# Count tables of the first mean layer stored in five parts, four pairs apart

## The chip, the cores and the metric

The kernel runs on one core of a Trainium2 chip. The metric is the time of one execution on the device in microseconds (us), the median of several runs. TensorE (PE in the profile), VectorE (DVE), ScalarE (ACT), GpSimd (POOL) and SyncE (SP) each follow their own list of instructions and meet in semaphores.

## What is computed

Four graph layers run one after the other on a graph of 3125 nodes with 128 features and 53125 edges sorted by destination: a gated layer, a mean layer, an attention pair and a pair of mean layers with normalisation. The change touches the second, whose sum over the edges is

```
deg = segment_sum(ones_like(dst), dst, n); deg = maximum(deg, 1.0)
agg = segment_sum(feat[src], dst, n)
h = feat @ W_self + b_self + agg / deg[:, None] @ W_neigh
x = layernorm(x + h)
```

The last two layers sum the same way, `segment_sum(x[src], dst)`, over the same edges.

## The kernel before, in words

**No gather, but counts.** The sum over edges is a product with a matrix that counts, for each source node and each destination node, the edges between them. Edges are sorted by destination, so a run of edges meets few destinations. The 104 batches of 512 edges are cut into pairs of 256 edges (208 pairs), and 26 pairs make one *table* (`SBP = 26`): for every source node (25 tiles of 128, `NT`) a row of 428 destination columns (`M_COLS`) in bf16. A table is 128 partitions x 25 x 428 values, 21400 bytes in each partition. There are 8 tables (`NSB`), the last one in two blocks of 18 and 8 pairs. Three tables fit on chip (`TABS = 3`, tile `counts`).

**The stage** is `mean_build` (L1677). For each pair n, VectorE makes one-hot matrices (`make_lo`, `make_wide`, `make_onto`, three pairs ahead), TensorE multiplies them (`count`, L1832 to L1835) into one of four banks, and ScalarE copies the bank into the table at the pair's own column (`copy_counts`, L1777 to L1783) and increments `copied`. A bank is free again when its copy is done, so TensorE can be some pairs ahead of ScalarE and no more. While table k is being counted, TensorE multiplies table k-1 with the features split in three bf16 parts (`apply`, L1850), some three matmuls after each pair, and VectorE adds the result to `acc` (`add_dense`, L1926, with a register load of the table's origin at L1920).

**Registers.** The column of each pair is known at run time only. ScalarE loads the 26 columns of a table into registers in one instruction (`loaded_starts`, L753 to L758, called at L1806 when `n % SBP == 0`):

```
if n % SBP == 0:
    values = loaded_starts(mybir.EngineType.Activation, place_m[0:1, n:n + SBP], M_COLS - WP)
```

The attention stage does the same with 14 columns a table (`place_a`), on ScalarE and on VectorE, beside the row gathers of GpSimd.

**The stores.** The last two layers need the same tables, so each one is written to DRAM (`count_tabs`) when it is finished, by `keep(s)` on SP (L1739 to L1741): it waits for `copied >= 26 (s+1)` and issues one transfer of 2675 KB, which increments `table_stored[s % 3]` by 16. ScalarE's `clear(k)` (L1767 to L1775) sets a column strip of the next table to zero in the middle of the table before; from the fourth table on it waits for the store of the table that had the buffer. The `update` stage that follows (L679 to L682) waits on SP for all stores. At the end of `mean_build` SP, TensorE and VectorE each load the value `rounds` (L1239).

Nothing else is issued on SP in the stage but three weight loads at its start. The order on each engine is the order in which the Python code issues; the semaphores do the rest. The names that the steps of the prediction use are `keep`, `clear`, `copy_counts`, `loaded_starts`, `place_m`, `copied` and `table_stored`.

Of the kernel before, what the change touches and what calls it, by code (L numbers as in the profile page):

```python
# [41 lines left out]
NSB, AT_DENSE = 8, 7  # L42
# [8 lines left out]
def build_program(nc, a, out):  # L51
# [9 lines left out]
    NT = -(-(N + W) // P)  # L61
# [127 lines left out]

    first_ad = dram("first_ad", [NB * BE + NODES, 1])  # L190
    count_tabs = dram("count_tabs", [NSB, P, NT * M_COLS], BF16)
    TABS = 3
    table_stored, table_in = [sem(f"table_stored{i}") for i in range(TABS)], [sem(f"table_in{i}") for i in range(2)]
    aux_rows = dram("aux_rows", [NB * BE, 4])
    tables = [dram(f"table{i}", [NODES, P]) for i in range(5)]
# [468 lines left out]
    def update(name):  # L664

        with phase(name) as (sb, sem):
            a_made, summed = sem("a_made"), sem("summed")
            v, normed, normed_d = sem("v"), sem("normed"), sem("normed_d")
            count, variance, root, deviation, by_act, by_dve, rstd_ready = norm_parts("n", sb, sem)
            w_n = wide_w[:, P:2 * P]  # L670
            ZB = 6

            def by_engine(g):

                return CHUNKS[1][0] <= g and (g - CHUNKS[1][0]) % 2 == 1

            with nc.Block() as block:  # L677
                @block.sync
                def _(sp):  # L679
                    clear_spent(sp)  # L680
                    for k in range(TABS):
                        sp.wait_ge(table_stored[k], 16 * len(range(k, NSB, TABS)))  # L682

                @block.tensor
                def _(pe):
                    for g in range(NG):
                        reach(pe, summed, tiles_to(g - ZB) if g >= ZB else 0)
                        for n, t in enumerate(GROUPS[g]):
                            mm = pe.matmul(bank[g % ZB][:, n * P:(n + 1) * P], acc[:, t * P:(t + 1) * P], w_n, start=True, stop=True)
                        mm.then_inc(a_made, 1)  # L690

                @block.scalar
                def _(act):
                    for c in range(2):
                        root(act, c)
                        act.wait_ge(rstd_ready, c + 1)
                        for g in range(*CHUNKS[c]):
                            if not by_engine(g):
                                for t in GROUPS[g]:
                                    by_act(act, x_sb, y_sb, t).then_inc(normed, 1)  # L700

                @block.vector
                def _(dve):
                    link = chain(dve, v)
                    def mean(g):
                        dve.wait_ge(a_made, g + 1)
                        for n, t in enumerate(GROUPS[g]):
                            dve.scalar_tensor_tensor(out=y_sb[:, t, :], in0=bank[g % ZB][:, n * P:(n + 1) * P],
                                                     scalar=rdeg[:, t:t + 1], in1=y_sb[:, t, :],
                                                     op0=ALU.mult, op1=ALU.add).then_inc(summed, 1)  # L710

                    def measure(g):
                        dve.wait_ge(summed, tiles_to(g))
                        count(dve, y_sb, g)

                    for g in range(NG):
                        mean(g)
                        if g >= 1:
                            measure(g - 1)
                            if g - 1 == CHUNKS[0][1] - 1:  # L720
                                variance(dve, link, 0)
                            elif g - 1 == CHUNKS[0][1]:
                                deviation(dve, link, 0)
                    measure(NG - 1)
                    variance(dve, link, 1)
                    deviation(dve, link, 1)
                    dve.wait_ge(rstd_ready, 2)
                    for g in range(*CHUNKS[1]):
                        if by_engine(g):
                            for t in GROUPS[g]:  # L730
                                by_dve(dve, x_sb, y_sb, t).then_inc(normed_d, 1)
# [945 lines left out]
    def mean_build(name, table, x_from, w_self, w_neigh, b):  # L1677

        with phase(name) as (sb, sem):
# [56 lines left out]
            with nc.Block() as block:  # L1736
                @block.sync
                def _(sp):
                    def keep(s):  # L1739
                        sp.wait_ge(copied, (s + 1) * SBP)  # L1740
                        sp.dma_start(count_tabs[s, :, :], flat(counts[:, s % TABS, :, :])).then_inc(table_stored[s % TABS], 16)  # L1741

                    clear_spent(sp)
                    sp.wait_ge(a_made, NG)
                    load_self(sp)
                    for s in range(NSB):
                        keep(s)
                    sp.wait_ge(flagged, 1)
                    with only_when(sp) as R:
                        store_rows(sp, table, x_from, tabled)  # L1750
                        fall_sp(sp, R)
# [13 lines left out]
                @block.scalar  # L1765
                def _(act):
                    def clear(k):  # L1767
                        first, _, width, at = M_BLOCKS[k]
                        s = home(first)
                        reach(act, applied, s - TABS + 1)  # L1770
                        if s >= TABS:
                            act.wait_ge(table_stored[s % TABS], 16 * (s // TABS))
                        rest_from, rest_to = at + width - REST, M_COLS if k < LEAP else at + width
                        act.copy(counts[:, s % TABS, :, rest_from:rest_to],
                                 zero[:, 0:1].rearrange("p (a b) -> p a b", a=1).broadcast_to([P, NT, rest_to - rest_from])).then_inc(cleared, 1)  # L1775

                    def copy_counts(n, values):  # L1777
                        act.wait_ge(counted, n + 1)
                        if opens(M_BLOCKS, n):
                            act.wait_ge(cleared, sum(block[0] <= n for block in M_BLOCKS))  # L1780
                        reach(act, copied, n)
                        act.copy(counts[:, home(n) % TABS, :, bass.ds(values[n % SBP], WP)],  # L1782
                                 BANKS_C[n % CR][:, 0:NT * WP].rearrange("p (t w) -> p t w", w=WP)).then_inc(copied, 1)  # L1783

                    def sigmoid(g):
                        act.wait_ge(summed, tiles_to(g))
                        act.activation(sig[:, cut(g), :], y_sb[:, cut(g), :], ACT.Sigmoid).then_inc(sig_ready, 1)

                    def normalise(g):
                        act.wait_ge(rstd_ready, 1 if g < CHUNKS[0][1] else 2)  # L1790
                        for t in GROUPS[g]:
                            by_act(act, x_from, y_sb, t).then_inc(normed, 1)

                    def cast_part(g, k):
                        if k == 0 and by_engine(g):
                            act.wait_ge(normed_d, normed_to(DVE_GROUPS, g))
                        elif k == 0:
                            act.wait_ge(normed, normed_to(ACT_GROUPS, g))
                        cast(act, g, k)

                    act.wait_ge(nothing, 1)
                    clear(0)
                    clears = {first + size // 2: k + 1 for k, (first, size, _, _) in enumerate(M_BLOCKS) if k + 1 < LAST}
                    for n in range(NDD):
                        if n % SBP == 0:
                            values = loaded_starts(mybir.EngineType.Activation, place_m[0:1, n:n + SBP], M_COLS - WP)  # L1806
                        if n in SPLIT_AT:
                            cast_part(*SPLIT_AT[n])
                        if n - 1 in SELF:
                            copy_self(act, SELF[n - 1])  # L1810
                        if n == CLEAR_AT:
                            act.copy(acc[:, :], zero[:, 0:1].broadcast_to([P, NODES])).then_inc(acc_clear, 1)
                        if n in clears:
                            clear(clears[n])
                        copy_counts(n, values)
                        if n < NG:
                            sigmoid(n)
                        if n in ROOT_AT:
                            root(act, ROOT_AT[n])
                        for g in NORMALISE.get(n, ()):  # L1820
                            normalise(g)
# [920 lines left out]
```

## Time and profile before

| what | us |
|---|---|
| median of 3 runs | 2037.59 (2037.51 to 2041.03) |
| the profiled execution, its own time | 2039.3 |
| its span | 2037.5 |
| granted clock of TensorE, mean | 0.91 |
| count stage with stores of tables | about 677 to 970 |
| first and last store issued | 741.4, 963.0 |

The span is the time from the first to the last instruction that the profiler recorded; the execution's own time is 1.8 us longer. Times inside the trace are us from the span's start. "Idle before" in a timeline stands in brackets behind an instruction, with what ended it; "issue" is time in which the engine waited for nothing that the profile shows. Register loads (TENSOR_LOAD) are not counted as busy, and stand under the engine's sequencer (ACTq, DVEq). A granted clock of 1.00 is 2.4 GHz, one of 0.50 is 1.2 GHz.

### The profile page before, as it was taken

To read this page: it belongs to the slowest core of one execution; us is meant where nothing else is said; L and a number is where in the kernel's file an instruction comes from. 1 tells how busy PE (TensorE), PEld (TensorE's weight loads), DVE (VectorE), ACT (ScalarE), POOL (GpSimd) and SP (SyncE) were. 2 spreads that over 40 slices of the span, in tenths; PEclk is the share of its full clock that TensorE was granted. 3 is DMA by queue.
4 is the path that set the end of the run, shared out by engine and by line. 5 is a ranking of instruction groups with operands and counts; after the bars stand their busy time and mean duration, and the time that the engine had idled before them with its cause. 6 is when DMAs were issued, how large, how long until landed. Compare 5 with 4: busy or idle time off the path is not lost. (4 is left out here: it accounts for less than half of the span.)

```text
span 2037.5 us, 42968 instructions
## 1 busy us (share of the span) xinstructions
PE 1742.0 (85%) x13651; PEld 1405.7 (69%) x13651; DVE 1412.8 (69%) x4286; ACT 911.7 (45%) x2490; POOL 983.6 (48%) x998
## 2 busy tenths in 40 slices
PE   5799999999999558888466999967599999299996
PEld 5699999999998425445464878757467878166664
DVE  5687788888886778885667766655676664744656
ACT  2566667676665266664303544421154453411100
POOL 3776777777774300000356777735577775300000
PEclk9799999999999759999768999986699999699998
DMA  6988788888884011222352111107221111344542
GB/s 191 269 241 240 235 240 255 256 249 246 255 255 148 7 55 55 109 109 89 127 143 62 45 41 43 45 15 200 70 67 41 41 43 37 123 162 180 198 163 87
DMA packets 145067, 276.87 MB, mean 136 GB/s; under 512 B 28295, under 2 KB 88333, under 8 KB 141556
## 3 DMA queue, kind: packets, MB, share of 16 engines
q1 hardware_dynamic: 104526, 191.58, 29.2%
q0 software_dynamic: 35456, 79.88, 14.5%
q10 hardware_dynamic: 4854, 2.55, 0.5%
q8 instruction: 118, 1.93, 0.4%
q14 instruction: 113, 0.93, 0.1%
HBM read 228.82 MB, written 45.08 MB: 134 GB/s over the span
## 5 line engine op out<-in xcount | busy, mean ns | idle before, releaser
L959 POOL DMA_INDIRECT gated_rows<-p_tab,src_idx x416 | 429.7, 1033 | 176.0 <-issue 104.4
L1351 POOL DMA_INDIRECT ring<-table,src_idx x384 | 384.1, 1000 | 146.4 <-issue 93.0
L2159 PE MATMUL bank<-counts,mean_xs 128*128 128x416 bf16 (+2 forms) x1350 | 219.5, 321 | 32.0 <-DVE mean_xs L1671 32.0
L1000 PE MATMUL bank<-gated_wide_q,gated_comb 128*128 128x256 f32 x832 | 216.8, 384 | 0.0
L1157 DVE TENSOR_TENSOR gated_pre<-bank,gated_rows 128x512 f32<-128x512 f32 x208 | 142.8, 687 | 101.8 <-PE bank L1000 101.8
L2159 PEld LDWEIGHTS bank<-counts,mean_xs 128*128 128x128 bf16 x1350 | 126.2, 98 | 116.1 <-issue 34.4
L1482 ACT COPY attention_counts<-bank 128x475 f32 (+1 forms) x224 | 127.2, 568 | 176.3 <-PE bank L1506 153.4
L1517 PEld LDWEIGHTS bank<-attention_counts,h_sb 128*128 128x128 f32 x900 | 157.5, 190 | 62.3 <-ACT attention_counts L1482 3.8
L1073 ACT ACTIVATE gated_sig<-gated_pre 128x512 f32<-128x512 f32 x208 | 131.1, 630 | 154.1 <-DVE gated_pre L1157 152.0
L1517 PE MATMUL bank<-attention_counts,h_sb 128*128 128x232 f32 (+1 forms) x900 | 191.9, 341 | 2.3 <-DVE attention_counts L1574 1.7
L1506 PE MATMUL bank<-attention_wide_b,scratch 128*128 128x400 f32 x448 | 189.5, 505 | 0.0
L1782 ACT CAST mean_counts<-bank 128x500 f32 x208 | 124.4, 598 | 103.5 <-PE bank L1835 48.7
L1505 PE MATMUL bank<-attention_wide_a,scratch 128*128 128x300 f32 x448 | 158.2, 435 | 11.6 <-DVE attention_wide_b L1566 5.7
L1000 PEld LDWEIGHTS bank<-gated_wide_q,gated_comb 128*128 128x128 f32 x832 | 143.5, 193 | 11.1
L1463 ACT ACTIVATE scratch<-scratch,w_tab 128x64 f32<-128x64 f32 x384 | 102.2, 336 | 102.1 <-DVE scratch L1551 102.1
L1850 PE MATMUL bank<-mean_counts,mean_xs 128*128 128x416 bf16 (+2 forms) x675 | 142.6, 332 | 3.3 <-ACT mean_counts L1782 2.7
L2345 POOL IOTA attend_spare_at<- 128x25 f32 x1 | 0.2, 162 | 282.2 <-POOLq L677 282.2
L1019 PE MATMUL bank<-gated_w,gated_siluT 128*128 128x128 f32 x832 | 126.4, 274 | 0.0
L1886 DVE TENSOR_TENSOR mean_lo<-lo_iota,src_lo 128x256 bf16<-128x256 bf16 x208 | 87.4, 420 | 46.7 <-PE bank L1835 46.2
L1557 DVE TENSOR_TENSOR scratch<-lo_iota,src_lo 128x256 f32<-128x256 bf16 x224 | 93.5, 418 | 33.4 <-PE bank L1506 23.6
L1032 PE MATMUL bank<-gated_hot,gated_msg 128*128 128x64 f32 x832 | 115.9, 262 | 0.1
L1574 DVE TENSOR_TENSOR attention_counts<-attention_counts,bank 128x25 f32 x206 | 40.5, 197 | 108.8 <-ACT attention_counts L1482 108.4
(428 smaller groups left out, 4018.7 us busy)
## 6 DMA issues: line engine op xcount, KB each, us to landing
counts<-count_tabs SPq DMA_DIRECT2D x16, 2675.0 KB, 9.9
h_sb<-in_edge_attr_dram SPq DMA_DIRECT2D x51, 512.0 KB, 4.9
count_tabs<-mean_counts SPq DMA_DIRECT2D x8, 2675.0 KB, 7.8
gated_relr<-rel_rows SPq DMA_DIRECT2D x104, 128.0 KB
gated_ids<-id_rows SPq DMA_DIRECT2D x26, 512.0 KB
gated_wide_q<-q_tab SPq DMA_DIRECT2D x208, 64.0 KB
attend_hot_lo<-low_hots SPq DMA_DIRECT2D x52, 256.0 KB, 3.3
gated_ea<-in_edge_attr_dram SPq DMA_DIRECT2D x51, 256.0 KB
```

Source lines behind the costliest of these rows:

```text
L959: pool.indirect_dma_start(out=rows[:, q % TICKS, c, :], out_offset=None, in_=p_tab, in_offset=bass.IndirectOffsetOnAxis(ap=src_idx[:, b, j ...
L1000: mm = pe.matmul(PRE[q % 2][:, c * 2 * P:(c + 1) * 2 * P], comb[:, u, k, c, :], wide_q[:, u, c, :], start=True, stop=True)
L1019: mm = pe.matmul(M[:, c * P:(c + 1) * P], siluT[:, q % 2, c, :], w2[:, :], start=False, stop=True, skip_group_check=True)
L1073: act.activation(flat(sig[:, q % 4, :, :]), flat(pre[:, q % 2, :, :]), ACT.Sigmoid).then_inc(sig_ready, 1)
L1157: dve.tensor_tensor(flat(pre[:, q % 2, :, :]), PRE[q % 2][:, :], flat(rows[:, q % TICKS, :, :]), ALU.add).then_inc(pre_ready, 1)
L1351: pool.indirect_dma_start(out=rows[:, n % RING, j, :], out_offset=None, in_=table, in_offset=bass.IndirectOffsetOnAxis(ap=src_idx[:, gathe ...
L1482: act.copy(counts[:, home(n), :, skip:A_COLS][:, :, bass.ds(values[n % ATP], WP - skip)], frm[:, :, skip:WP]).then_inc(copied, 1)
L1505: pe.matmul(to[:, :, 0:WA], lo[:, n % LR, 0, :], wide_a[:, n % WR, :], start=True, stop=False, skip_group_check=True)
L1506: pe.matmul(to[:, :, OFF:WP], lo[:, n % LR, 1, :], wide_b[:, n % WR, :], start=False, stop=True, skip_group_check=True).then_inc(counted, 1)
L1517: mm = pe.matmul(BANKS_D[k % 2][:, 0:width], h_sb[:, m, :], counts[:, home(first), m, at:at + width], start=(m == 0), stop=(m == NT - 1), ...
L1850: mm = pe.matmul(BANKS_D[k % 2][:, 0:width], xs[:, m // 3, m % 3, :], counts[:, home(first) % TABS, m // 3, at:at + width], start=(m == 0) ...
L2159: mm = pe.matmul(BANKS_D[q % ND][:, 0:width], xs[l][:, m // 3, m % 3, :], counts[:, s % 2, m // 3, at:at + width], start=(m == 0), stop=(m ...
```

## The change

A table is stored in five transfers of five node tiles each (535 KB, 4280 bytes in each partition). Part i waits for `copied >= 26 (s+1) + 4 i`, or for all 208 pairs if that is less, so the first part is issued where the whole table was, and the others 4, 8, 12 and 16 copies later, while the next table is being filled. A finished table now counts 80 on its semaphore.

```diff
--- before.py
+++ after.py
@@ -189,7 +189,9 @@
 
     first_ad = dram("first_ad", [NB * BE + NODES, 1])
     count_tabs = dram("count_tabs", [NSB, P, NT * M_COLS], BF16)
-    TABS = 3
+    TABS, PARTS, APART = 3, 5, 4
+    assert NT % PARTS == 0
+    STORED = 16 * PARTS
     table_stored, table_in = [sem(f"table_stored{i}") for i in range(TABS)], [sem(f"table_in{i}") for i in range(2)]
     aux_rows = dram("aux_rows", [NB * BE, 4])
     tables = [dram(f"table{i}", [NODES, P]) for i in range(5)]
@@ -679,7 +681,7 @@
                 def _(sp):
                     clear_spent(sp)
                     for k in range(TABS):
-                        sp.wait_ge(table_stored[k], 16 * len(range(k, NSB, TABS)))
+                        sp.wait_ge(table_stored[k], STORED * len(range(k, NSB, TABS)))
 
                 @block.tensor
                 def _(pe):
@@ -1737,8 +1739,11 @@
                 @block.sync
                 def _(sp):
                     def keep(s):
-                        sp.wait_ge(copied, (s + 1) * SBP)
-                        sp.dma_start(count_tabs[s, :, :], flat(counts[:, s % TABS, :, :])).then_inc(table_stored[s % TABS], 16)
+                        for i in range(PARTS):
+                            sp.wait_ge(copied, min((s + 1) * SBP + APART * i, NDD))
+                            part = slice(i * NT // PARTS, (i + 1) * NT // PARTS)
+                            sp.dma_start(count_tabs[s, :, part.start * M_COLS:part.stop * M_COLS],
+                                         flat(counts[:, s % TABS, part, :])).then_inc(table_stored[s % TABS], 16)
 
                     clear_spent(sp)
                     sp.wait_ge(a_made, NG)
@@ -1769,7 +1774,7 @@
                         s = home(first)
                         reach(act, applied, s - TABS + 1)
                         if s >= TABS:
-                            act.wait_ge(table_stored[s % TABS], 16 * (s // TABS))
+                            act.wait_ge(table_stored[s % TABS], STORED * (s // TABS))
                         rest_from, rest_to = at + width - REST, M_COLS if k < LEAP else at + width
                         act.copy(counts[:, s % TABS, :, rest_from:rest_to],
                                  zero[:, 0:1].rearrange("p (a b) -> p a b", a=1).broadcast_to([P, NT, rest_to - rest_from])).then_inc(cleared, 1)
```

The order of SP's queue in this stage before the change (the rows are DMA issues and what follows them; `rounds` is the value loaded at the stage's end):

```order
L769 DMA wide_w<-in_L_gnn_W_neigh_dram 128x128
L770 DMA wide_w<-in_L_gnn_b_self_dram 128x128
L1741 DMA count_tabs<-mean_counts 128x10700 [waits mean1_copied] x8
L1239 TENSOR_LOAD rounds [waits mean1_flagged]
L1240 COMPARE_AND_BRANCH
```

And with the change:

```order
L771 DMA wide_w<-in_L_gnn_W_neigh_dram 128x128
L772 DMA wide_w<-in_L_gnn_b_self_dram 128x128
L1745 DMA count_tabs<-mean_counts 128x2140 [waits mean1_copied] x40
L1241 TENSOR_LOAD rounds [waits mean1_flagged]
L1242 COMPARE_AND_BRANCH
```

Eight stores of 10700 values in each partition became forty of 2140; what stands before and behind them is the same. On the other engines no instruction is added, taken away or moved.

## Rows read from the trace of the kernel before

**Rows 1.** The page: span and busy time of the engines, whole program.
```profile
span 2037.5 us, 42968 instructions
PE 1742.0 (85%) x13651; PEld 1405.7 (69%) x13651; DVE 1412.8 (69%) x4286; ACT 911.7 (45%) x2490; POOL 983.6 (48%) x998
```

**Rows 2.** Windows from one store of a table to the next (us from the start).
```profile
core 0: us, PE busy (x) PEld busy (x) DVE busy (x) ACT busy (x) POOL busy (x), PEclk, DMA share, GB/s
815.40:846.80 31.40, 23.48 (x152) 13.36 (x152) 23.34 (x96) 16.79 (x27) 0.00 (x0) 0.89 0.21 89
846.80:869.90 23.10, 22.15 (x152) 12.65 (x152) 22.62 (x93) 16.64 (x27) 0.00 (x0) 1.00 0.29 120
```

**Rows 3.** Waits in the count stage, 735 to 985 us: in total, times, longest.
```profile
ACT mean_counts L1782 <- issue: 39.4, 4, 9.9
PE bank L1832 <- ACT mean_counts L1782: 21.8, 3, 7.6
```

**Rows 4.** Timelines of ACT, then PE, 814 to 828 us: start, length, instruction, idle before.
```profile
825.23 0.57 ACT L1782 CAST mean_counts<-bank 128x500 f32 x1 [9.86 <-issue]
...
826.06 0.20 PE L1832 MATMUL bank<-mean_onto,mean_lo 128*128 128x25 bf16 x1 [7.55 <-ACT mean_counts L1782]
```

**Rows 5.** Loads of place_m on ACT (xcount, ns min/median/max): all from 735 us, then the first.
```profile
L755 ACTq TENSOR_LOAD <-place_m x7: 2698/10141/10264, 740.8 to 923.4; - x7
...
L755 ACTq TENSOR_LOAD <-place_m x1: 10222/10222/10222, 740.8 to 740.8; - x1
```

**Rows 6.** Timeline of SP's queue: the store of the third table.
```profile
815.40 0.32 SPq L1741 DMA_DIRECT2D count_tabs<-mean_counts  x1
```

**Rows 7.** Windows inside a long register load (740.8 on) and a short one (788.9).
```profile
740.80:742.20 1.40, 0.79 (x4) 0.27 (x3) 1.40 (x7) 0.57 (x1) 0.00 (x0) 0.50 0.00 0
742.20:748.90 6.70, 2.03 (x8) 0.66 (x6) 2.67 (x12) 0.00 (x0) 0.00 (x0) 0.75 0.97 409
788.90:790.20 1.30, 0.00 (x0) 0.00 (x0) 1.30 (x6) 0.00 (x0) 0.00 (x0) 1.00 1.24 527
```

**Rows 8.** Loads of one value on DVE, all and two of them; first load of place_m.
```profile
L1920 DVEq TENSOR_LOAD <-origin_m x9: 302/889/912, 794.5 to 963.7; - x9
...
L1920 DVEq TENSOR_LOAD <-origin_m x2: 302/303/304, 954.9 to 956.5; - x2
...
L755 ACTq TENSOR_LOAD <-place_m x1: 1933/1933/1933, 677.5 to 677.5; - x1
```

**Rows 9.** Attention stage: ACT's second and third load of place_a.
```profile
L755 ACTq TENSOR_LOAD <-place_a x1: 3037/3037/3037, 1113.6 to 1113.6; - x1
...
L755 ACTq TENSOR_LOAD <-place_a x1: 1236/1236/1236, 1146.3 to 1146.3; - x1
```

**Rows 10.** DMA issues, page and 1000 to 1090 us: count, KB, us to landing.
```profile
count_tabs<-mean_counts SPq DMA_DIRECT2D x8, 2675.0 KB, 7.8
...
table<-h_sb SPq DMA_DIRECT2D x2, 576.0 KB, 3.9
```

**Rows 11.** Register loads of rounds, 960 to 975 us.
```profile
L1239 SPq TENSOR_LOAD <-rounds x1: 511/511/511, 963.4 to 963.4; - x1
...
L1239 PEldq TENSOR_LOAD <-rounds x1: 916/916/916, 966.8 to 966.8; - x1
L1239 DVEq TENSOR_LOAD <-rounds x1: 927/927/927, 968.4 to 968.4; - x1
```

**Rows 12.** Windows after two idles of PE, and the shorter idle in PE's timeline.
```profile
774.80:778.20 3.40, 3.40 (x15) 2.63 (x16) 0.68 (x3) 1.03 (x2) 0.00 (x0) 0.50 0.00 0
...
822.60:826.00 3.40, 0.00 (x0) 0.00 (x0) 0.00 (x0) 0.60 (x2) 0.00 (x0) 0.50 0.00 0
826.00:829.40 3.40, 3.34 (x14) 1.64 (x15) 1.85 (x7) 2.75 (x5) 0.00 (x0) 0.50 0.02 5
829.40:832.80 3.40, 3.40 (x27) 2.09 (x26) 2.92 (x13) 2.36 (x5) 0.00 (x0) 1.00 0.01 2
...
774.79 1.43 PE L800 MATMUL bank<-wide_w,cur 128*128 128x128 f32 x5 [2.75 <-ACT cur L793]
```

## Prediction

> **What bounds the kernel now.** I read the page first: 2037.5 us of span, TensorE busy 85% [rows 1]. Section 4 traces only the end of the program, so I went to the stage that is changed. The windows by table come next [rows 2]: the time from one store of a count table to the next alternates between 31.4 and 23.1 us, for the same 26 pairs and the same TensorE work (23.48 us busy and 22.15 us). So every second table loses 8.3 us. In the short ones TensorE (22.15 of 23.10) and VectorE (22.62) are both nearly full: those have nothing to give. The loss is named in the list of waits of this stage [rows 3]: ScalarE's copy of counts stands 39.4 us, in 4 idles of about 9.9 us, on "issue", which is nothing that the list can name. Its timeline [rows 4] shows one of them: the copy that opens a table starts at 825.23 after 9.86 us of idle, and TensorE starts again at 826.06, after 7.55 us, waiting for ScalarE.
>
> What fills the 9.86 us is a register load, the TENSOR_LOAD of 26 values of `place_m` at L755, which the loop on ScalarE makes when n is a multiple of 26 [rows 5]. There are seven such loads after the first; the median is 10141 ns, the most 10264, the least 2698. With seven of them and the median at 10141, four are long, and four idles are listed: those that open tables 1, 3, 5 and 7, counted from 0 (the one of table 1 took 10222 ns; I take 10.2 us). Those that open 2, 4 and 6 took 2.7 us.
>
> The store of the table just finished is issued by the same event, the 26th copy: SP issues it at 815.40 [rows 6], where ScalarE's idle begins (825.23 less 9.86 us). The windows around the first long load [rows 7] show the transfer: nothing from 740.8 to 742.2, then 6.7 us at 409 GB/s with all 16 DMA engines taken (share 0.97), and 6.7 x 409 is 2.74 MB, the whole table, so it is over at 748.9. The load runs from 740.8 to 751.1 and holds that transfer whole. My reading is that **a register load advances slowly while the transfer runs**.
>
> Other register loads speak for it [rows 8]. VectorE's loads of one value, `origin_m`, of which one follows behind most stores, take 889 ns in the median and 912 at most, and 304 ns at 954.9, where nothing moves. And the first load of 26 values, at 677.5 without a transfer, takes 1933 ns, where the equally short ones take 2698 ns with the last 1.3 us of them in a transfer (the one that ends at 790.2, with a transfer from 788.9 [rows 7]).
>
> **How long would a long load be alone?** No row has it, so I bound it. From below: 1.4 us of it lie ahead of the transfer and 2.2 us behind it [rows 7], so at least 3.6 us. From above: 10.2 us. The nearest rows are the attention stage's loads of 14 values, which alternate in the same phase: 3037 ns at the second, 1236 ns at the third [rows 9]; the program's offsets are 56 bytes times an odd or even number there, 104 bytes times the same here. With 0.30 us for one value, another costs (3.04 - 0.30)/13 = 0.211 us at odd places and (1.24 - 0.30)/13 = 0.072 at even ones; the load at 677.5 gives (1.93 - 0.30)/25 = 0.065 for even ones with no transfer about, 10% less than beside the gathers of the attention stage. So the long load alone is 0.30 + 25 x 0.211 = 5.6 us, or 5.1 us with the 10% taken off. I take **5.4 us**. The stretch is then 10.2 - 5.4 = 4.8 us in 6.7 us of transfer, 0.72 us for each.
>
> The Trainium skill (Runtime: NRT & Kernel Launch, section Instruction fetch mechanics) gives about 200 ns a register for such a load; by that one it would be 5.2 us, the saving per load below 4.0 us in place of 3.8, and the sum 16 us. The row of 1933 ns for 26 values contradicts it for even offsets.
>
> **The change, part by part.**
> 1. The first fifth of a table is stored where all of it was, at the same copy. A fifth is 535 KB; at the measured 409 GB/s it moves in 1.34 us. It starts and hits the load where the whole did, and stretches it by 1.34 x 0.72 = 0.96 us. The load is then 5.4 + 1.0 = 6.4 us, and 3.8 us less than 10.2.
> 2. That load is on the path: TensorE's idle of 7.55 us is the load less 2.7 us that its three spare banks cover, and the table is 8.3 us longer for it [rows 2, 4]. After the change TensorE's idle is about 6.4 - 2.7 = 3.7 us. **4 loads x 3.84 us = 15.4 us.**
> 3. The three short loads have 1.3 us in a transfer. The first fifth covers just that: nothing gained, nothing lost.
> 4. The four further fifths start 4, 8, 12 and 16 copies later, about 3.5 us apart in a short table. They are on SP's queue; the load holds ScalarE, so no copy is counted before it ends, and none of these can meet it. No other register load of ScalarE lies there. VectorE's one-value loads (9 of them, median 889 ns [rows 8]) mostly come some 1.8 us after the store, when the first fifth is nearly through; each may be 0.3 us shorter, and between 0 and 2 us in all would follow. I take 0, since the last of the fifth may still meet them.
> 5. Costs: 32 more issues on SP. One issue takes 0.33 us [rows 6], and SP has nothing else to do in this stage; the order of rows shows it queues only the load of `rounds` behind them. ScalarE's clears wait on `table_stored`, now for the last fifth: that is issued 16 copies later, and the clear that wants the buffer comes 39 copies after the first, so some 23 copies (20 us) remain for a transfer that lands in 7.8 us at full size [rows 10]. Nothing.
> 6. The last table: all five waits are at 208, so five transfers start together where one did. TensorE's and VectorE's loads of `rounds` (916 and 927 ns [rows 11]) fall into them as before. SP's own load, 511 ns at 963.4, comes some 2 us later and ends before TensorE's at 966.8. Nothing.
> 7. TensorE's clock. In the idle of 7.55 us it falls to 0.50 at 822.6, for 6.8 us, of which 3.4 are idle and 3.4 work: 14 matmuls at 0.50, 27 at 1.00, a loss of 1.6 us [rows 12]. After an idle of 2.75 us (ends 774.79) it stands at 0.50 for 3.4 us, all of it on work (15 matmuls). An idle of 3.7 us lies between. If it falls as it ends, for 3.4 us, the cost is the same as now, and I take 0. Bounds: no fall, 1.6 us less for each of 4; or 6.8 us at half all on work, 1.6 us more for each.
>
> Sum: 2037.5 - 15.4 = 2022.1 us of span. The profiled execution took 2039.3 us, its span and 1.8 us around it; the median of the three runs is 2037.59, and against it I forecast **2022.2 us**.
>
> The Trainium skill (DMA: Bandwidth & Descriptors, section Bandwidth) speaks against the edit: it wants transfers of 1 MiB or more for three quarters of the peak, and 535 KB is under that. The row at hand is a store of 576 KB, which lands in 3.9 us [rows 10], where 2675 KB take 7.8.
>
> **Ends of the range.** From that row: a full store lands 1.1 us after its 6.7 us of moving, so 576 KB move in 2.8 us at most. With that and the long load at 5.6 alone (stretch 4.6/6.7 = 0.69 a us), it would be 7.5 us and 2.7 saved, 10.8 in all; with the clock's worse bound (+6.4) that is 2033. At the other end reads stand still in a transfer, the load alone is 3.6 us, 6.6 x 0.8 = 5.3 us are saved each time, 21.1 in all: 2016.5, and with the clock's better bound (-6.4) 2010. Both ends at once on either side are unlikely: I give **2013 to 2031**.
>
> **Rivals.**
> - *Reads stand still during a transfer* (0.09): 2016.5 us. For it: the four long loads are alike. Against: the short load ended at 790.2, in the midst of a transfer that began at 788.9 [rows 7].
> - *The shorter idle costs as much clock* (0.08): 6.8 us at half lie wholly on work; 2022.2 + 6.4 = 2028.6 us.
> - *The change doesn't do what it says* (0.05): the loads are long by their odd offset alone, transfer or not, and keep 10.2 us; TensorE waits as before: 2037.6 us. Against: 14 values at odd offsets take 3.04 us, and 25 of 0.211 make 5.6 us, not 10.2; VectorE's 889 against 304 ns.
> - *Slower* (0.03): a fifth takes as long as a whole, because its cost lies in its pieces (one per partition, 4280 bytes in place of 21400) and not in its bytes. Then a table's five take 33.5 us of transfer while a table lasts 27.2 on average (the mean of a long and a short one), the first fifth still spans the load (nothing saved), and the stores fall behind until ScalarE's clears wait for the buffer: the fifth table's last part would end 5 x 33.5 = 167.5 us after the first store, and is wanted after 5 x 27.2 + 13.6 = 149.6 us. That is 18 us late: 2055.6 us. It decides from (149.6/25 =) 6.0 us a fifth. The 3.9 us landing of 576 KB speaks against it.
>
> The forecast's own case keeps 0.75. All chances but the last two are faster by over 0.2% (4.1 us, about what a measurement of this kernel tells from no change): faster 0.92, within 0.05, slower 0.03.
>
> **What the profile after would show.** The four long loads of `place_m` at 6.4 us (5.0 if reads stand still, 10.2 if nothing helps), the three short ones still at 2.7; ScalarE's idle on "issue" down from 39.4 to about 24 us; TensorE's four idles at 3.5 to 4.5 us; long tables of 27.5 us beside short ones of 23; five bursts of some 1.3 us a table, 40 issues landing in 2.5 to 4 us. I am wrong if the long loads stay over 8 us, if the clock stands at half for more than 4 us of work behind each, or if a later stage gives the gain back.

## The result and the profile after

| what | before | with the change |
|---|---|---|
| median of the runs compared, us | 2038.10 (5 runs) | 2025.19 (5 runs, 2022.09 to 2027.98) |
| ratio | | 0.9927, 95% interval 0.9906 to 0.9949 |
| span of the profiled execution, us | 2037.5 | 2023.9 |

The forecast was 2022.2 us in a range of 2013 to 2031. A later comparison of the same kernel gave 2020.24 us and a ratio of 0.9912 (0.9897 to 0.9926). The whole interval lies below 0.998 both times: faster. Ratios, here and below, compare executions in the chip's normal state alone; one execution of the last kernel below took 6199 us, for a reason that nothing here shows, and its ratio leaves it out.

The page of the kernel after, span and busy times, against [rows 1]: the engines do the same work as before, in 13.6 us less.

```profile
span 2023.9 us, 43000 instructions
PE 1743.0 (86%) x13651; PEld 1407.0 (70%) x13651; DVE 1414.0 (70%) x4286; ACT 912.9 (45%) x2490; POOL 982.3 (49%) x998
```

Windows from one store's first issue to the next, against [rows 2] (columns as there):

```profile
core 0: us, PE busy (x) PEld busy (x) DVE busy (x) ACT busy (x) POOL busy (x), PEclk, DMA share, GB/s
816.26:843.91 27.65, 23.54 (x152) 13.37 (x152) 23.45 (x97) 16.81 (x27) 0.00 (x0) 0.94 0.25 101
843.91:866.91 23.00, 22.06 (x152) 12.65 (x152) 22.92 (x95) 16.64 (x27) 0.00 (x0) 1.00 0.30 120
866.91:894.51 27.60, 23.54 (x152) 13.36 (x152) 22.37 (x92) 16.93 (x27) 0.00 (x0) 0.94 0.25 100
894.51:917.37 22.86, 21.87 (x152) 12.81 (x152) 22.54 (x94) 16.61 (x27) 0.00 (x0) 1.00 0.30 122
917.37:950.63 33.26, 30.38 (x222) 19.72 (x223) 21.25 (x80) 16.70 (x27) 0.00 (x0) 1.00 0.21 84
```

The short tables last 23.0 and 22.86 us, as before. The long ones have gone from 31.4 to 27.65 and 27.60 us. The last window is that of the last table, which is counted in two blocks; the same window of the kernel before, not among the rows above, is:

```profile
924.07:963.05 38.98, 32.26 (x222) 20.35 (x223) 21.69 (x82) 16.66 (x27) 0.00 (x0) 0.91 0.17 72
```

It is 5.7 us shorter, and its clock is 1.00 for 0.91.

Waits of the count stage, against [rows 3]:

```profile
ACT mean_counts L1787 <- issue: 24.2, 4, 6.1
PE bank L1837 <- ACT mean_counts L1787: 11.1, 4, 3.8
```

ScalarE's idle on "issue" fell from 39.4 to 24.2 us, TensorE's wait for ScalarE in this list from 21.8 (3 waits) to 11.1 (4 waits, the fourth of 0.7 us). TensorE's idle at the first of the four tables stands in another row, that of the copy `cur`: 8.17 us before, 4.62 after. The timelines of ScalarE and TensorE at the same table, against [rows 4]:

```profile
822.26 0.58 ACT L1787 CAST mean_counts<-bank 128x500 f32 x1 [6.03 <-issue]
...
823.09 0.18 PE L1837 MATMUL bank<-mean_onto,mean_lo 128*128 128x25 bf16 x1 [3.72 <-ACT mean_counts L1787]
```

6.03 us in place of 9.86, and 3.72 in place of 7.55. The register loads of `place_m`, and below them VectorE's of one value, against [rows 5, 8] (count, ns least/median/most):

```profile
L757 ACTq TENSOR_LOAD <-place_m x7: 2618/6365/6435, 745.6 to 916.7; - x7
...
L1925 DVEq TENSOR_LOAD <-origin_m x9: 301/441/562, 795.4 to 951.3; - x9
```

The median load of ScalarE is 6365 ns where it was 10141, the least 2618 where it was 2698. VectorE's loads are 441 ns in the median for 889. Windows around the first long load, which starts at 745.6, and around two of TensorE's idles, against [rows 7, 12], and the shorter of these idles in TensorE's timeline:

```profile
745.60:746.90 1.30, 0.69 (x4) 0.19 (x3) 1.30 (x7) 0.58 (x1) 0.00 (x0) 0.50 0.00 0
746.90:748.40 1.50, 1.50 (x8) 0.72 (x6) 1.50 (x7) 0.00 (x0) 0.00 (x0) 0.56 0.91 365
747.20:748.10 0.90, 0.90 (x5) 0.49 (x4) 0.90 (x4) 0.00 (x0) 0.00 (x0) 0.50 1.03 414
...
823.30:826.70 3.40, 3.40 (x14) 1.63 (x13) 1.86 (x7) 2.68 (x5) 0.00 (x0) 0.50 0.25 93
921.30:924.20 2.90, 0.05 (x1) 0.03 (x1) 0.62 (x3) 0.64 (x2) 0.00 (x0) 1.00 0.00 0
924.20:927.60 3.40, 3.39 (x24) 2.04 (x25) 2.51 (x10) 2.43 (x5) 0.00 (x0) 1.00 0.08 31
...
924.21 0.18 PE L1837 MATMUL bank<-mean_onto,mean_lo 128*128 128x25 bf16 x1 [2.86 <-ACT mean_counts L1787]
```

The first fifth moves in 1.5 us, from 1.3 us after the load's start (second row: 1.5 us at 365 GB/s are its 548 thousand bytes), where the whole table took 6.7. In the middle of it (third row) it moves at 414 GB/s, as fast as the whole table did (409). The fourth row is 3.4 us of work at half clock after the idle that ends at 823.09. The last rows are the idle of 2.86 us at the last long load and the stretch behind it: clock 1.00, no fall. Last, the issues and the end of the stage, against [rows 6, 10, 11]:

```profile
count_tabs<-mean_counts SPq DMA_DIRECT2D x40, 535.0 KB, 2.7
...
950.63 4.17 SPq L1745 DMA_DIRECT2D count_tabs<-mean_counts  x5
...
L1241 PEldq TENSOR_LOAD <-rounds x1: 915/915/915, 954.3 to 954.3; - x1
L1241 SPq TENSOR_LOAD <-rounds x1: 1089/1089/1089, 954.9 to 954.9; - x1
...
L1241 DVEq TENSOR_LOAD <-rounds x1: 924/924/924, 956.0 to 956.0; - x1
```

Forty stores land in 2.7 us in the median. The last five are issued over 4.17 us, and SP's load of `rounds` comes behind them at 954.9.

### The profile page after: what moved, and what is told of

Same layout as the page of the kernel before. It is cut to its first block and busy times, and to the rows that moved or that the text cites. A ratio compares the mean times of both kernels' runs of the same rounds, so it can differ in the third digit from the quotient of the medians.

```text
span 2023.9 us, 43000 instructions
## 1 busy us (share of the span) xinstructions
PE 1743.0 (86%) x13651; PEld 1407.0 (70%) x13651; DVE 1414.0 (70%) x4286; ACT 912.9 (45%) x2490; POOL 982.3 (49%) x998
## 3 DMA queue, kind: packets, MB, share of 16 engines
q8 instruction: 118, 1.93, 0.4%
## 5 line engine op out<-in xcount | busy, mean ns | idle before, releaser
L1012 PEld LDWEIGHTS bank<-ae_v,gated_eaT 128*128 128x128 f32 x832 | 110.6, 194 | 0.0
```

## The experiments

Four kernels ran first, each one edit away from the kernel before or after, and four more after them. "Idle" is TensorE's at the opening of a table.

**The whole store, four copies later.** Only the wait of the kernel before is moved; the transfer stays one of 2675 KB.

```diff
-                        sp.wait_ge(copied, (s + 1) * SBP)
+                        sp.wait_ge(copied, min((s + 1) * SBP + 4, NDD))
```

> The kernel before, with the one store of a table issued 4 copies later (at copy 26(s+1)+4), so that no transfer meets ScalarE's register load. Theory (a load is stretched by the transfer that runs beside it): from 10.22 us with 6.7 us of transfer and 6.41 us with 1.5 us of it, the long loads alone come out at 5.3 us and the short ones at 1.95 us; TensorE's four idles fall to about 2.6 us, 4.9 us are saved at each of four tables, and the time is about 2018 us (0.990 of before), better than the five parts though the store is whole. Rival (it is the spreading over the table that helps): the whole transfer hurts wherever it stands, and the time stays at 2030 us or above. Rival (long by their odd offset alone): loads of 10.2 us, 2038 us.

Measured: 2017.31 us, ratio 0.9892 (0.9869 to 0.9915). The profile of this kernel: loads of `place_m` and `origin_m`, then TensorE's timeline at the second and the third long load, then the windows of the second long load and of its transfer:

```profile
L755 ACTq TENSOR_LOAD <-place_m x7: 1931/5543/5586, 744.1 to 908.6; - x7
...
L1920 DVEq TENSOR_LOAD <-origin_m x9: 300/305/559, 791.9 to 942.2; - x9
...
817.77 0.18 PE L1832 MATMUL bank<-mean_onto,mean_lo 128*128 128x25 bf16 x1 [2.90 <-DVE mean_wide_b L1894]
...
866.91 0.18 PE L1832 MATMUL bank<-mean_onto,mean_lo 128*128 128x25 bf16 x1 [2.89 <-ACT mean_counts L1782]
...
811.00:816.80 5.80, 3.86 (x25) 1.91 (x23) 5.80 (x25) 0.62 (x1) 0.00 (x0) 1.00 0.00 0
816.80:825.00 8.20, 7.22 (x40) 4.00 (x41) 5.90 (x24) 5.97 (x11) 0.00 (x0) 0.79 0.59 251
```

The long loads take 5.54 us (median), the short ones 1.93, VectorE's 0.305. The idle is 2.90 us, and 2.89 at the next long load; the first of these waits is put down to VectorE's matrix, the second to ScalarE's copy. The DMA share is 0.00 during the load and 0.59 after it. So the change's own parts, their size and their spacing, are not what helps: a store in one piece does at least as well if it starts behind the load. This run also measures what no row of before had: **the long load alone, 5.54 us**.

**Five parts, all at once.**

```diff
-    TABS, PARTS, APART = 3, 5, 4
+    TABS, PARTS, APART = 3, 5, 0
```

> The five parts of the change, but all five issued at the same copy, where the whole store was before. Theory (the time that a transfer runs beside the load is what counts): the transfer lasts 6.7 us again, the long loads are back at about 10.2 us, 2038 us (1.000 of before). Rival (shorter pieces, 4280 bytes in place of 21400 for each partition, let the register reads in between): loads of 6.4 us, and the time of the change, 2025 us.

Measured: 2038.84 us, ratio 0.9997 (0.9986 to 1.0009). Loads, TensorE's idle at the third table and the issues, in its profile:

```profile
L757 ACTq TENSOR_LOAD <-place_m x7: 2698/10303/10437, 741.9 to 925.0; - x7
...
825.96 0.20 PE L1837 MATMUL bank<-mean_onto,mean_lo 128*128 128x25 bf16 x1 [7.69 <-ACT mean_counts L1787]
...
count_tabs<-mean_counts SPq DMA_DIRECT2D x36, 535.0 KB, 4.6
```

Loads of 10.30 us and an idle of 7.69 us: the gain is gone with the same forty transfers. Short pieces do not let the register reads in: five transfers that run one behind the other for 6.8 us (743.3 to 750.1, at 402 GB/s) stretch the load as the whole one does.

**Two parts, eight copies apart.**

```diff
-    TABS, PARTS, APART = 3, 5, 4
-    assert NT % PARTS == 0
+    TABS, PARTS, APART = 3, 2, 8
```

> The change with 2 parts (12 and 13 node tiles) 8 copies apart: the first part is 1.31 MB, 3.2 us of transfer. Theory (stretch in proportion to the transfer's time, 0.75 us a us on 5.3 us): long loads of 7.7 us, short ones 2.7 us, time about 2028 us (0.995). Rival (reads stand still until the transfer is over, or there is a fixed charge for each transfer met): the load is not on that line, by 0.5 us or more.

Measured: 2028.75 us, ratio 0.9948 (0.9931 to 0.9965). Its loads, and the window of the first part's transfer:

```profile
L756 ACTq TENSOR_LOAD <-place_m x7: 2652/7685/7823, 744.7 to 918.5; - x7
...
745.80:749.00 3.20, 1.87 (x8) 0.74 (x6) 2.92 (x13) 0.00 (x0) 0.00 (x0) 0.80 0.98 411
```

Four points now, from 5.54 us: 1.5 us of transfer gave 6.37 (0.55 us a us), 3.2 us gave 7.69 (0.67), 6.7 us gave 10.14 in the kernel before (0.69) and 10.30 with five at once (0.71). It is close to a line, with a smaller slope for the shortest. A fixed charge for each transfer met can be 0.04 us at most, since five transfers cost the load 0.16 us more than one of the same bytes. As all of these transfers run at about 400 GB/s, the runs do not tell whether the time beside the load counts or the bytes: a million bytes stretch it by 1.5, 1.6 and 1.7 us.

**Loads that begin at a multiple of four values.** The kernel before with its store in its old place; the loads of odd tables take two more values in front, which are dropped.

```diff
-                            values = loaded_starts(mybir.EngineType.Activation, place_m[0:1, n:n + SBP], M_COLS - WP)
+                            back = n % 4
+                            values = loaded_starts(mybir.EngineType.Activation, place_m[0:1, n - back:n + SBP], M_COLS - WP)[back:]
```

> The kernel before with its whole store where it was, but the loads of an odd table begin two values (8 bytes) earlier and take 28 values, so that each begins at a multiple of 4 values. Theory (the long loads are long because of an offset that is no multiple of 16 bytes, and so meet the whole transfer): all seven loads take 2.7 to 3.1 us, TensorE's idles of 7.5 us vanish, every table takes 23 us, and the time is about 2006 us (0.985): 4 times 7.5 us, and the clock's 6 us less at most. Rival (the alternation has another cause, as the tables' number or buffer): long loads stay at 10.2 us or above, 2038 us.

Measured: 2003.58 us, ratio 0.9831 (0.9814 to 0.9847). Loads, the one idle that is left at a table's opening, and two neighbouring tables from store to store:

```profile
L755 ACTq TENSOR_LOAD <-place_m x7: 1869/1972/2747, 741.8 to 895.5; - x7
...
780.65 1.65 PE L800 MATMUL bank<-wide_w,cur 128*128 128x128 f32 x6 [2.23 <-ACT cur L793]
...
804.94:827.42 22.48, 22.07 (x152) 12.44 (x152) 22.48 (x94) 16.80 (x27) 0.00 (x0) 1.00 0.30 124
827.42:850.54 23.12, 22.15 (x152) 12.56 (x152) 23.12 (x97) 16.63 (x27) 0.00 (x0) 1.00 0.28 120
```

The four loads of odd tables, now of 28 values, take 1.87 to 1.97 us, less than the 2.7 to 3.1 expected; the three of even tables, with 26 values, still take 2.7. Two neighbouring tables last 22.5 and 23.1 us. The alternation came from where the loads begin. It gains 35 us, where the change gained 13, because it removes the load's length and with it the time it can spend beside a transfer.

**The kernels of before and after, profiled again.** In the first profiles the stages ahead of the count stage, which the change does not touch, took 4.8 us more with it: ScalarE's first load started at 682.2 us for 677.5, its second at 745.6 for 740.8.

> The kernel before, unchanged, for a second profile: does the gated layer ahead of the count stage vary from one execution to the next? In the first profile ScalarE's first load of place_m starts at 677.5 us, in that of the change at 682.2. Theory (these 4.8 us are the spread of that layer between executions and no effect of the change): in this profile the first load starts anywhere from 677 to 683 us, while the count stage from the second load to VectorE's load of rounds takes 227 to 229 us again. Rival (the change makes the earlier layer slower): 677.5 us again within 0.5.

Measured: 2034.2 us, one run. Its first load of `place_m`, and VectorE's load of `rounds` at the stage's end:

```profile
L755 ACTq TENSOR_LOAD <-place_m x1: 1956/1956/1956, 678.2 to 678.2; - x1
...
L1239 DVEq TENSOR_LOAD <-rounds x1: 922/922/922, 966.2 to 966.2; - x1
```

And TensorE's second idle of its first long table, with the window behind it:

```profile
773.83 1.16 PE L800 MATMUL bank<-wide_w,cur 128*128 128x128 f32 x8 [2.76 <-ACT cur L793]
...
773.83:777.23 3.40, 3.40 (x26) 2.49 (x27) 1.84 (x5) 1.92 (x4) 0.00 (x0) 1.00 0.00 0
```

> The changed kernel, unchanged, for a second profile and more times. Theory (spread of the gated layer): the first load of place_m starts anywhere from 677 to 683 us, the count stage from the second load to VectorE's load of rounds takes 210 to 211 us again, the long loads 6.4 us, the time 2020 to 2026 us. Rival (the change makes the earlier layer slower): 682 us or later again.

Measured: 2020.24 us, ratio 0.9912 (0.9897 to 0.9926). The same rows of it, with the seven loads between:

```profile
L757 ACTq TENSOR_LOAD <-place_m x1: 1957/1957/1957, 678.1 to 678.1; - x1
...
L757 ACTq TENSOR_LOAD <-place_m x7: 2666/6379/6456, 740.9 to 909.9; - x7
...
L1241 DVEq TENSOR_LOAD <-rounds x1: 934/934/934, 949.2 to 949.2; - x1
```

The first load starts at 678.2 in the one and 678.1 in the other: the 4.8 us came from the execution, not from the change. From the second load to VectorE's `rounds` the stage takes 225.2 us (741.0 to 966.2) and 208.3 us (740.9 to 949.2), 16.9 less; in the first pair of profiles it was 227.6 (740.8 to 968.4) and 210.4 (745.6 to 956.0), 17.2 less. Both stages came out 2 us below what I had written for the theory, and by the same amount. The difference lies in the table of the first long load: from its load to the next one it lasts 44.3 us for 46.7 in the kernel before, 40.6 for 42.8 in that of the change. TensorE's clock recovered sooner there, and it stayed at 1.00 behind the idle of 2.76 us, where the same idle of the same kernel was followed by half clock in the first profile [rows 12].

**Both repairs together.** The two edits above, the load's start and the later store, on the kernel before.

> Both repairs on the kernel before: the loads of odd tables begin two values earlier (28 values), and the one store is issued 4 copies later. Theory: all seven loads take 1.7 to 1.95 us, VectorE's loads of one value 0.3 us. TensorE had already no idle at the tables with even loads alone (a load under 2.7 us is covered by its spare banks), so this adds no more than VectorE's 5 x 0.6 us: 2001 to 2004 us (0.982). Rival (each load is on the path in full): another 3 x 0.8 us and more, 1999 us or below.

Measured: 1999.07 us, ratio 0.9806 (0.9791 to 0.9821). Its loads and the idle at the second table:

```profile
L755 ACTq TENSOR_LOAD <-place_m x7: 1717/1740/1944, 743.7 to 893.1; - x7
...
781.36 1.16 PE L800 MATMUL bank<-wide_w,cur 128*128 128x128 f32 x8 [1.44 <-ACT cur L793]
```

The loads are as expected, 1.72 to 1.94 us. The time is below the range of the theory, 2001 to 2004 us, and at the bound of the rival, 1999. The intervals of this kernel and of even loads alone (0.9814 to 0.9847) overlap, so a gain beyond it is likely but not certain. The profiles name a place that I had put at nothing: the idle of 2.23 us at 780.65, where TensorE waits not for a count but for a copy that ScalarE makes right behind the load, has no cover of banks; it is 1.44 us here, 0.79 less, for a load of 1.94 us in place of 2.74. So the short loads are not free at every table. The same idle is there before and after the change, with 2.20 us in both.

**The attention stage's loads too.** As the last kernel, and on ScalarE and VectorE:

```diff
-                                values = loaded_starts(mybir.EngineType.Activation, place_a[0:1, n:n + ATP], A_COLS - WP)
+                                back = n % 4
+                                values = loaded_starts(mybir.EngineType.Activation, place_a[0:1, n - back:n + ATP], A_COLS - WP)[back:]
...
-                            values = loaded_starts(mybir.EngineType.DVE, place_a[0:1, n:n + ATP], A_COLS - WP)
+                            back = n % 4
+                            values = loaded_starts(mybir.EngineType.DVE, place_a[0:1, n - back:n + ATP], A_COLS - WP)[back:]
```

> As even_late, and the attention stages' loads of place_a on ScalarE and VectorE begin at a multiple of 4 values too (16 values for 14 in odd tables). Theory: the loads of 3.0 and 3.2 us fall to 1.1 us there as well, but TensorE is busy 31 of 32 us of each table of that stage and idles 1 us or less at the loads, so the time is that of even_late within 0.1%. Rival (eight loads of 2 us are on the path): 8 to 16 us less.

Measured: 1998.99 us over six executions, 1998.25 without the one of 6199 us, ratio 0.9803 (0.9790 to 0.9816). ScalarE's loads of `place_a` in the first attention stage, all and the second:

```profile
L755 ACTq TENSOR_LOAD <-place_a x8: 1012/1126/1402, 1043.5 to 1265.9; - x8
...
L755 ACTq TENSOR_LOAD <-place_a x1: 1027/1027/1027, 1071.6 to 1071.6; - x1
```

The second load fell from 3037 ns [rows 9] to 1027, and the time stayed within 1 us of the kernel without that edit. TensorE's idle behind that load was 0.98 us without the edit (it ends at 1074.85), and 0.96 us with it (1073.59). The same repair is worth nothing where TensorE does not wait for the engine that loads.

## Why the prediction was right

The time, 2025.19 us, is 3 us above the forecast, and the second comparison, 2020.24 us, 2 us below it. By its own steps:

1. **The long load alone.** I took 5.4 us between 3.6 and 10.2, from the rate of another stage's loads [rows 9]. Late store: 5.54 us. My unreduced figure, 5.6, was the better one; the 10% that I took off for the gathers was not there. It came from dividing by values: counted by reads, as the last section does, the aligned loads beside the gathers and without them cost the same, 1.24/5 = 0.25 and 1.93/8 = 0.24 us.
2. **The stretch by the first fifth.** Forecast 0.96 us and a load of 6.4 us; the median is 6.37 us. The parts missed and made up for each other, which is luck: the load alone is 5.54 us for 5.4, and the stretch 0.83 us for 0.96, from 1.5 us of transfer for 1.34 (365 GB/s over it with its start and end, in place of 409) at 0.55 us a us for 0.72.
3. **The load is on the path.** Forecast idle 3.7 us at each; the four are 4.62, 3.72, 3.79 and 2.86 us, where they were 8.17, 7.55, 7.51 and 6.69: 3.6 to 3.8 us less each time, 14.9 in all. The banks' cover of 2.7 us was right for the middle two alone: the load less the idle is 1.7, 2.7, 2.6 and 3.6 us. Tables of 27.6 us for 27.5. Right, and the three runs that set the load to 5.5, 7.7 and 10.3 us moved the time with it, to 2017, 2029 and 2039 us.
4. **Short loads: no gain and no loss.** 2.62 to 2.72 us for 2.70: right for this change. But not every short load is free: at the second table TensorE idles 2.20 us behind it before and after, and the run with both repairs gained there.
5. **VectorE's loads.** I took 0 and said up to 0.3 us each; they fell by 0.45 us in the median. It shows in no table's length: the short tables stayed at 23.0 us.
6. **The end of the stage.** I said that SP's load of `rounds` would end before TensorE's. It did not: the five issues, of 0.32 to 1.20 us each, took 4.17 us for the 2 I allowed, and it ran from 954.9 for 1.09 us, behind TensorE's (954.3 and 0.92). VectorE's was later than both, at 956.0, so it cost nothing.
7. **The clock.** I took 3.4 us of work at half clock behind each idle, as before. It was so at 823.3. After the last and shortest idle (2.86 us, and 2.88 in the second profile) there was no fall, where there had been one in both profiles of the kernel before (idles of 6.69 and 6.64 us). That table took 33.26 us for 38.98: 5.7 us less, of which 3.8 are the load's; the rest fits the 1.6 us that I gave for one fall spared, and TensorE's busy time in that window is 1.9 us less. I had put this term at nothing; it is the one that was mis-sized: the stage saved 17.2 and 16.9 us where the sum had 15.4.

The span fell by only 13.6 us because the execution profiled for the change had lost 4.8 us in a stage ahead of it; the second pair of profiles shows 17.3 (2032.4 and 2015.1). Whether the other four executions of the first comparison, whose median gained 12.9 us where the second gained 18.5, lost time in the same place is not known: they have no profile. That the forecast of 15.4 lies between the two is in part luck.

The rivals: reads that stand still in a transfer meant long loads of 3.6 us alone and 5.0 with the change, and they take 5.54 and 6.37; a load that is long by its offset alone is refuted by the late store, though the aligned load, which meets the same store in 1.9 to 2.7 us, shows that the offset has the larger part in it; the dearer clock and the slow small pieces did not come. The Trainium skill's figure of 200 ns for a register (Runtime: NRT & Kernel Launch, section Instruction fetch mechanics) agrees with the long loads alone, 5.54 us for 26 values or 0.21 each, and is three times what the aligned ones take, 1.93 us or 0.07 each. The Trainium skill speaks of such loads from HBM (same page, section Terms), and `place_m` lies on chip. The Trainium skill's rule on transfers of 1 MiB and more (DMA: Bandwidth & Descriptors, section Bandwidth) did not show: the first fifth moved at 365 GB/s over its 1.5 us, nine tenths of the 409 of the whole store, and no wait in the lists of this stage ends on a store.

## What to carry to other kernels

A large transfer is not free because its bytes wait for nobody: look at what else is triggered by the event that issues it. Here a load of runtime offsets into registers started at that same event, and what helped was to keep the two apart, not to cut the transfer; moving one wait gave at least as much as five parts. And where a wait is stretched, ask first why it is long: the values read from a 16-byte boundary took a third of the time, which was worth 35 us, and nothing in the stage where the loading engine had slack.

## What the runs showed of the hardware

- The time of a register load does not go by its values. Alone, 26 values of an odd table, which begin 8 bytes past a multiple of 16, take 5.54 us, 26 of an even table, which begin at a multiple of 16 bytes, 1.93 us, and 28 that begin there 1.72 to 1.74 us: more values, less time. The 14 and 16 values of `place_a` fit it: 14 reads 3.04 us, 5 reads 1.23 us, 4 reads 1.03 us. This rule is an inference from these loads; only these two places of a start were run, and that the tile itself begins at such a boundary is taken from the fit too.
- A read beside a running transfer takes longer: VectorE's one value 0.30 us alone and 0.89 us beside it. What holds it up was not tested.
- Five issues of 535 KB in a row took 4.17 us on SP (4.20 in the run with all five at once), 0.32 us the shortest and 1.20 the longest, where I had expected 2 us. Why they grow was not tested.
- TensorE's granted clock was 0.50 behind an idle of 2.75 us [rows 12] and 1.00 behind the same idle, 2.76 us, in the second profile of the same kernel; with the store four copies later it was 0.53 over the 3.4 us behind the idle of 2.90 us and 1.00 behind that of 2.89. The length of one idle does not decide it, so its cost at one place can differ from one execution to the next.
